# Seven scans ahead of the attention, attention from slot 7, and the feed-forward behind it, in a kernel of two fused layers

## What is computed

```python
xn = layernorm(x)
# layer 0: a selective scan ...
hs, gate = split(xn @ in_proj_w.T)                 # 256 + 256
u  = silu(conv4(hs) + conv_b)
dt, Bm, Cm = rmsnorm of the three parts of u @ x_proj_w.T   # 64, 16, 16
dt = softplus(dt @ dt_proj_w.T + dt_proj_b)
h_t = exp(dt_t * A) * h_{t-1} + (dt_t * u_t) * B_t  # 256 channels x 16 states, over 512 tokens
y  = (sum over states of h * C + u * D) * silu(gate)
x  = x + y @ out_proj_w.T + moe(xn)                 # ... and 8 experts, the best one for each token
xn = layernorm(x)
# layer 1: sliding-window attention (16 heads of 8, |i - j| <= 32) and a gated feed-forward
x  = x + attention(xn) @ Wo + bo + (silu(xn @ wg.T) * (xn @ wu.T)) @ wd.T   # 384 hidden
```

## Time and profile before

| | |
|---|---|
| median of 3 runs | 1098.06 us (1095.71 to 1100.03) |
| profiled execution | 1103.31 us |
| its span | 1101.5 us |
| PE busy | 850.0 us (77%) |
| DVE busy | 763.1 us (69%) |
| ACT busy | 648.3 us (59%) |
| POOL busy | 434.4 us (39%) |
| scans (DVE, 128 of them) | 291.8 us, 2280 ns each |
| mean granted TensorE clock | 0.879 |

### The profile page before, as it was taken

The page is one execution under the profiler, slowest core; times in us unless marked ns, Lnnn a source line. Parts: engine busy times, 40 slices in busy tenths (PEclk is TensorE's granted clock), DMA queues, the critical chain, the costliest instruction groups (busy, mean ns, idle before and its releaser), DMA issues.

```text
span 1101.5 us, 15596 instructions
## 1 busy us (share of the span) xinstructions
PE 850.0 (77%) x5226; PEld 576.7 (52%) x5226; DVE 763.1 (69%) x1059; ACT 648.3 (59%) x1985; POOL 434.4 (39%) x241
## 2 busy tenths in 40 slices
PE   1953888785888878886888787987888788789685
PEld 0731877673644564455445554664456445554443
DVE  7566344556668856895679667856797679878476
ACT  0231556553577637763676567655785577578474
POOL 2256312205732373336433643256226622763000
PEclk9757999986888989998989888898899889889898
DMA  6454888864432442325323542344234423451000
GB/s 226 135 180 124 235 264 272 249 184 96 107 78 68 87 132 70 88 62 143 79 75 79 129 96 63 87 115 104 67 83 117 105 65 82 117 129 40 21 11 10
DMA packets 85951, 123.19 MB, mean 112 GB/s; under 512 B 8560, under 2 KB 43760, under 8 KB 85744
## 3 DMA queue, kind: packets, MB, share of 16 engines
q1 hardware_dynamic: 79584, 115.38, 38.6%
q0 software_dynamic: 6288, 6.82, 2.7%
HBM read 106.21 MB, written 12.29 MB: 108 GB/s over the span
## 4 chain that ended last, share of the span: by engine, by line
PE 40%; DVE 18%; issue 17%; POOL 14%; ACT 8%; DMA 2%; SPq 0%; POOLq 0%; DVEq 0%; ACTq 0%
DVE hst L826 7%; PE more L1451 6%; PE y_bank L1319 6%; POOL hc L1224 6%; PE work L1465 3%; POOL xs_d L1192 3%; PE work L1338 3%; DVE dBu L818 3%; POOL x_res L1208 2%; PE work_l L1433 2%; ACT pexp L1122 2%; PE work L1344 2%; PE work L1364 1%; PE work L1290 1%; PE work L1433 1%
## 5 line engine op out<-in xcount | busy, mean ns | idle before, releaser
L1224 POOL TENSOR_TENSOR hc<-hst,bcr 128x1024 f32<-128x1024 f32 x116 | 281.8, 2429 | 493.2 <-DVE dBu L818 493.2
L826 DVE TENSOR_TENSOR_SCAN hst<-dA,dBu 128x1024 f32<-128x1024 f32 x128 | 291.8, 2280 | 3.3 <-ACT dA L1046 1.8
L1319 PE MATMUL y_bank<-pk,hc 128*128 128x128 f32 x1024 | 154.0, 298 | 54.0 <-POOL hc L1224 50.4
L818 DVE TENSOR_TENSOR dBu<-dtu,bcr 128x1024 f32<-128x1024 f32 x128 | 163.8, 1280 | 35.0 <-DMA bcr<-bc_d 25.7
L1046 ACT ACTIVATE dA<-dt,neg_a 128x511 f32<-128x511 f32 x256 | 170.3, 726 | 12.4 <-DVE hst L826 9.2
L1319 PEld LDWEIGHTS y_bank<-pk,hc 128*128 128x128 f32 x1024 | 126.2, 153 | 89.6 <-POOL hc L1224 60.7
L1451 PE MATMUL more<-pk,pexp 128*96 128x128 f32 x480 | 110.5, 301 | 73.7 <-ACT pexp L1122 68.0
L1451 PEld LDWEIGHTS more<-pk,pexp 128*96 128x96 f32 x480 | 58.9, 129 | 123.4 <-issue 87.8
L1122 ACT ACTIVATE pexp<-work,nmax 128x96 f32<-128x96 f32 x240 | 78.4, 341 | 35.5 <-DVE nmax L973 35.3
L1135 ACT COPY pT<-more 96x512 f32<-96x512 f32 x120 | 69.9, 583 | 44.6 <-PE more L1451 44.3
L1122 ACT ACTIVATE pexp<-work_l,nmax 128x96 f32<-128x96 f32 x240 | 78.1, 340 | 16.5 <-DVE nmax L973 16.4
(11 more groups left out here) (355 smaller groups left out, 1543.4 us busy)
## 6 DMA issues: line engine op xcount, KB each, us to landing
bcr<-bc_d SPq DMA_DIRECT2D x128, 512.0 KB
qbd<-in_wx SPq DMA_DIRECT2D x8, 578.0 KB
o_all<-in_wx SPq DMA_DIRECT2D x8, 578.0 KB
pT<-in_wx SPq DMA_DIRECT2D x8, 578.0 KB
kT<-in_wx SPq DMA_DIRECT2D x8, 578.0 KB, 5.5
vw<-in_wx SPq DMA_DIRECT2D x8, 578.0 KB, 5.7
xs_d<-rbuf POOLq DMA_DIRECT2D x1, 2560.0 KB, 9.7
hst<-in_hidden SPq DMA_DIRECT2D x8, 256.0 KB, 6.6
```

Of the source, the lines that this page charges most:

```text
L818: v.tensor_tensor(dBu[:], dtu[par], bcr[n % RING][:, 0:1, :].to_broadcast([P, NH, L]), ALU.mult).then_inc(s_dBu, 1)
L826: v.tensor_tensor_scan(hst[n % 2][:].rearrange("p h t -> p (h t)"), dA[n % 2][:].rearrange("p h t -> p (h t)"), dBu[:].rearrange("p h t -> ...
L1224: g_.tensor_tensor(hc[n % 2][:], hst[n % 2][:], bcr[n % RING][:, 1:2, :].to_broadcast([P, NH, L]), ALU.mult).then_inc(s_hc, 1)
L1319: last = t.matmul(y_bank[h][:, q], hc[n % 2][:, h, q], ident, is_transpose=True, start=False, stop=(n == N - 1 and j == NT - 1))
```

## The change

The first scans stand in slots 0 to 6, one each, and the others in 8, 10, 12, 14, 16, 18, 20, 23 and 25. Attention begins in slot 7. `HEAD` is gone: the second halves `sg` and `drl` stand in `REST`, a slot after their first halves. The feed-forward stands in slots 24 to 27, and takes the banks of attention (0, 1, 2) in place of bank 5; `fg` k now waits for `fs` k - 1, and `fs` k for `fh` k - 1. The sixteen transfers of `own_heads` are issued four at a time after steps 0 to 3, and the denominators' after the last four. The transfer of k (`kin`) stands a slot later than k, xdbl two slots earlier, the indirect additions into x_res (`rows`) in slots 9 to 15 in place of 5 to 11. The load of ScalarE's ln table is a unit, `ln_set`, in slot 18. The plan of the last turn is unchanged.

```diff
@@ -66,27 +66,26 @@
-ATTN_AT = 10
-STEP_AT = (0, 1, 3, 4, 6, 8, 10, 12, 14, 16, 17, 19, 21, 22, 24, 26)
+ATTN_AT = 7
+STEP_AT = (0, 1, 2, 3, 4, 5, 6, 8, 10, 12, 14, 16, 18, 20, 23, 25)
-HEAD = {11: [("pre", "sg0", 0)], 12: [("pre", "sg1", 0)], 15: [("pre", "drl0", 0)], 16: [("pre", "drl1", 0)],
-        18: [("attn", "fs", 0)], 19: [("attn", "fh", 0)], 20: [("attn", "fs", 1)], 21: [("attn", "fh", 1)],
-MID = {3: [("scan", "slots", 0)], 8: [("pre", "ss", 0)], 19: [("pre", "dw", 0)], 24: [("pre", "dt", 0)], 26: [("pre", "dtu", 0)]}
-REST = {1: [("attn", "x1", 0)],
+MID = {3: [("scan", "slots", 0)], 8: [("pre", "ss", 0)], 20: [("pre", "dw", 0)], 23: [("pre", "dt", 0)], 25: [("pre", "dtu", 0)]}
+REST = {1: [("attn", "x1", 0), ("attn", "ln_a", 0)],
+        4: [("attn", "kin", 0), ("pre", "th1", 0), ("pre", "u1", 0), ("attn", "v0", 0), ("attn", "v1", 0)],
+        24: [("attn", "fg", 0), ("attn", "fu", 0)],
+        25: [("attn", "fs", 0), ("attn", "fh", 0), ("attn", "fg", 1), ("attn", "fu", 1)],
+        26: [("attn", "fs", 1), ("attn", "fh", 1), ("attn", "fg", 2), ("attn", "fu", 2)],
+        27: [("attn", "fs", 2), ("attn", "fh", 2), ("attn", "rden", 0), ("pre", "start", 0)]}
...
@@ -212,9 +208,9 @@
             "values": ["oL" if k == G - 1 else "oK"], "proj": [f"fin{k}"] if k >= 2 else []}.get(name, [])
 
 
-L1_BANK = {"yT0": 1, "yT1": 2, "out": 0, "xnT": 1, "q": 0, "k": 1, "v0": 2, "v1": 0, "v2": 1, "v3": 2, "rdT": 2, "fin": 0,
+L1_BANK = {"yT0": 1, "yT1": 2, "out": 0, "xnT": 1, "q": 0, "k": 1, "v0": 2, "v1": 0, "v2": 1, "v3": 0, "rdT": 2, "fin": 2,
            **{f"s{k}": k % 2 for k in range(G)}, **{f"pT{k}": 2 for k in range(G)},
-           "oL": 0, **{f"gate{k}": 5 for k in range(HC)}, **{f"up{k}": 5 for k in range(HC)}}
+           "oL": 0, "gate0": 1, "up0": 2, "gate1": 0, "up1": 1, "gate2": 2, "up2": 0}
 LAST_BANK = {"yT0": 1, "yT1": 2, "out": 0, "xnT": 1, "q": 3, "k": 4, "v0": 2, "v1": 6, "v2": 7, "v3": 5,
              **{f"s{k}": (0, 1, 3, 4)[k % 4] for k in range(G)}, **{f"pT{k}": (2, 6)[k % 2] for k in range(G)},
              "oK": 0, "oL": 1, **{f"gate{k}": 5 for k in range(HC)}, **{f"up{k}": 7 for k in range(HC)}, "fin2": 5, "fin3": 7}
@@ -481,11 +476,6 @@
 
         def take0(eng, b, key):
             before(eng, s_free0, b * L0_N + L0_USES.index(key))
-            at = BANK0.index(("pre", key))
-            lane, last = BANK0[at - 1]
-            a = b - LAG["attn"] + LAG["pre"] - (at == 0)
-            if lane == "attn" and 0 <= a < B:
-                done1(eng, a, FFN_KEY[last])
 
         def done0(eng, b, key):
             eng.wait_ge(s_free0, b * L0_N + L0_USES.index(key) + 1)
@@ -501,13 +491,6 @@
 
         def take1(eng, b, key):
             before(eng, free1(b, key), l1_before(b, key, l1_bank(b, key)))
-
-        def pre_done(eng, b, name):
-
-            lane, last = BANK0[BANK0.index(("attn", name)) - 1]
-            a = b + LAG["attn"] - LAG["pre"]
-            if lane == "pre" and a < B:
-                done0(eng, a, last)
 
         def done1(eng, b, key):
             if b >= 0:
@@ -602,21 +585,21 @@
                 rows = bc_d[b:b + 1].rearrange("o (k n) t -> o n k t", k=2)
                 sp.dma_start(bcr[n % RING][:], rows[:, n, :, :].to_broadcast([P, 2, L])).then_inc(s_bcr[n % RING], 16)
 
-            def own_heads(b):
-                done1(sp, b, f"gate{HC - 1}")
-                done1(sp, b, "oL")
-                for r in range(RG):
-                    for h in range(4):
-                        q = slice(32 * r + HD * h, 32 * r + HD * h + HD)
-                        sp.dma_start(o_own[q, :], o_all[q, h, :, :].rearrange("p g q -> p (g q)")).then_inc(s_own, 16)
+            def own_head_rows(b, r):
+                if r == 0:
+                    done1(sp, b, f"gate{HC - 1}")
+                    done1(sp, b, "oL")
+                for h in range(4):
+                    q = slice(32 * r + HD * h, 32 * r + HD * h + HD)
+                    sp.dma_start(o_own[q, :], o_all[q, h, :, :].rearrange("p g q -> p (g q)")).then_inc(s_own, 16)
+
+            def averages_of(b):
                 done1(sp, b, "rdT")
                 for r in range(RG):
-                    rows = rd_d[b, r] if isinstance(b, int) else rd_d[bass.ds(b, 1), r].rearrange("o h g q -> (o h) g q")
-                    sp.dma_start(rows.rearrange("h g q -> g h q"), rdenT[r * G:(r + 1) * G, :, :]).then_inc(s_rdst, 16)
+                    sp.dma_start(rd_d[b, r].rearrange("h g q -> g h q"), rdenT[r * G:(r + 1) * G, :, :]).then_inc(s_rdst, 16)
                 sp.wait_ge(s_rdst, b * 64 + 64)
                 before(sp, s_out, b * 16)
-                rows = rd_d[b:b + 1] if isinstance(b, int) else rd_d[bass.ds(b, 1)]
-                sp.dma_start(rd_rows, rows.rearrange("o r h g q -> (o r h) (g q)").unsqueeze(1).to_broadcast(
+                sp.dma_start(rd_rows, rd_d[b:b + 1].rearrange("o r h g q -> (o r h) (g q)").unsqueeze(1).to_broadcast(
                     [RG * 4, HD, L])).then_inc(s_rdin, 16)
 
             def body(it, par):
@@ -631,16 +614,20 @@
                             bc_rows(b, n)
                     if name == "spread" and k + RING - 1 < N:
                         bc_rows(b, k + RING - 1)
-                    if name == "spread" and k == 0 and b >= 2:
-                        own_heads(b - 2)
+                    if name == "spread" and k < RG and b >= 2:
+                        own_head_rows(b - 2, k)
+                        if k == RG - 1:
+                            averages_of(b - 2)
                     if name == "xnT" and (not isinstance(b, int) or b + 1 < B):
                         full0(sp, b, "xnT")
                         sp.wait_ge(s_xast[b + 1], 16)
                         sp.dma_start(x_in[:], seq(xn_d, b + 1)).then_inc(s_xin, 16)
                     if name == "rdT":
                         if b == B - 2:
-                            own_heads(b)
-                    if name == "k" and b < B - 1:
+                            for r in range(RG):
+                                own_head_rows(b, r)
+                            averages_of(b)
+                    if name == "kin":
                         if b == 0:
                             sp.wait_ge(s_clear, 1)
                         done1(sp, b, "k")
@@ -979,6 +966,8 @@
                     v.reciprocal(rden[:], den[:]).then_inc(s_rden, 1)
                 elif name == "fs":
                     dve.wait_ge(s_fth, b * HC + k + 1)
+                    if k > 0:
+                        done1(dve, b, f"up{k - 1}")
                     v.scalar_tensor_tensor(fsg[:], fth[:], 1.0, w1k(b, f"gate{k}")[:], ALU.add,
                                            ALU.mult).then_inc(free1(b, f"gate{k}"), 1)
                 elif name == "fh":
@@ -1076,6 +1065,8 @@
                     act.wait_ge(s_dab, b * NH + NH)
                     done0(act, b, "hs1")
                     s.activation(de, dab, ACT.Exp, scale=-1.0).then_inc(s_de, 1)
+                elif name == "ln_set":
+                    s.preload_act_table_set("natural_log_exp_and_others")
                 elif name == "dln":
                     act.wait_ge(s_dw, b + 1)
                     s.activation(dln, dw, ACT.Ln).then_inc(s_dln, 1)
@@ -1135,9 +1126,9 @@
                     s.copy(pT[k % 4][:], w1k(b, f"pT{k}")[0:KW, :]).then_inc(free1(b, f"pT{k}"), 1)
                 elif name == "fg":
                     full1(act, b, f"gate{k}")
+                    if k > 0:
+                        done1(act, b, f"gate{k - 1}")
                     s.activation(fth[:], w1k(b, f"gate{k}")[:], ACT.Tanh).then_inc(s_fth, 1)
-                    if k == HC - 1 and b < B - 1:
-                        s.preload_act_table_set("natural_log_exp_and_others")
                 elif name == "averages":
                     full1(act, b, "oL")
                     s.copy(o_all[:, :, G - O_LAG:G, :].rearrange("p h g q -> p g h q"),
@@ -1460,8 +1451,6 @@
                 elif name in ("fg", "fu"):
                     key, j = (f"gate{k}", 0) if name == "fg" else (f"up{k}", 1)
                     take1(pe, b, key)
-                    if b < B - 1:
-                        pre_done(pe, b, f"{name}{k}")
                     t.matmul(w1k(b, key)[:], ffn[:, j, k * P:(k + 1) * P], xn1T[:, WIN:WIN + L], start=True,
                              stop=True).then_inc(s_full1, 1)
                 elif name == "rdT":
```

28 lines of the change are left out of this document (10 added, 18 removed).

## The result

The changed kernel takes 1041.66 us (median of 4 runs, 1039.19 to 1043.19), the kernel before 1096.91 in the same job (1095.71 to 1100.03): the ratio is 0.949, 95% interval 0.9461 to 0.9519, some 55 us faster. I had said 1065. The profiled execution took 1043.19 us (span 1041.4), 60.1 less in span than the one of before, where my sum had 33 less.

What follows compares the result with a forecast made beforehand. No engine full; a serial loop through four engines bounds the middle. A turn 37.3 + 52 + 19.1 = 108.4 us; six turns -31, turn 7 -1.4, turn 0 -1.2, together -33: 1065 us, own range 1044 to 1087, 8-in-10 range 1036 to 1100.

Steps and rivals of the forecast that it cites:

- Stretch 1: Slots 0 to 7 with seven scans: 37.3 us, its end set by TensorE, the seventh scan filling VectorE's idle time.
- Stretch 2: Slots 8 to 22, seven scans among the attention's pairs: 52 us, bounds 48 and 56.
- The clean pairs: Middle slots' pairs without feed-forward or other extras, scans 5.16 us apart: 7.5 of them, 38.7 us.
- The preparation with nothing recovered: Middle slots: preparing the next sequence adds 14.7 us to 38.7, 53.4 with no waits of the second halves saved.
- My 11.2 us: The feed-forward's cost between the attention's pairs: 52.5 less 41.3 us, read from turn 7.
- Stretch 3: Slots 23 to 27, from the fifteenth scan to the next turn's first: a VectorE chain of 19.1 us, bounds 18 and 21.
- The clock: TensorE idling in slots 25 to 27 may start the next turn at 1.2 GHz: 0 to 2 us a turn, taken 0.
- Turns -1 and 0: Start of the kernel: turn 0, beside the experts, gains 1.2 us from scan 4; turn -1 unchanged, within 2.
- Turn 7: Last attention turn, preparing nothing: from 88.7 to 87.3 us, -1.4, with product 7's late rows not hidden.
- The loop that keeps 4.2 us a slot: Rival: the four-engine loop sets the attention slots' pace; middle 63 us, turn 119.4, kernel 1136 us; chance 0.12.
- The gap-free TensorE: Rival: TensorE becomes the bound without gaps; 101 to 102 us a turn, kernel 1026 us; chance 0.08.
- The gain spent in tail and start: Rival: clock, a longer tail and late first scores use up the gain; 112 to 114 a turn, 1090 to 1102 us; chance 0.15.

Runs made afterwards that it cites:

- scan7_in_attention: The changed kernel with the seventh scan moved back to slot 8, among the attention's pairs: 1063.7 us, ratio 0.968.
- row7_first: The changed kernel with k's shifted copies (kin) one slot later, in slot 5, behind the transfer of bcr's row 7: 1042.7 us, ratio 0.950.
- halves_ahead: The changed kernel with the second halves of gate and time step back ahead of the next slot's scan, first halves moved too: 1071.7 us, ratio 0.975.
- ffn_middle: The changed kernel with the feed-forward back between the attention's pairs (slots 18 to 24) on its shared bank: 1057.0 us, ratio 0.962.
- eight_scans: The changed kernel with x_dbl in slot 7, kin in slot 5 and the eighth scan in slot 7, ahead of the pairs: 1038.9 us, ratio 0.947.
- filler: eight_scans plus sixteen identity matmuls ahead of pair 11's transposes in each of six turns: 1034.2 us, ratio 0.942.
- xdbl_slot7: The changed kernel with only the x_dbl projection moved from slot 5 back to slot 7: 1036.6 us, ratio 0.944.
- seven_load_later: The changed kernel with x_dbl back in slot 7 and the logarithm's table load in slot 19, seven scans kept ahead: 1034.0 us, ratio 0.942.
- table_load_later: eight_scans with ScalarE's load of the logarithm's table one slot later, in slot 19: 1033.0 us, ratio 0.941.

## Why the prediction was too small

The sign and the mechanism of the packed scans were right; the sizes were not. By parts, predicted and measured in span: to sequence 1 -1.2, -10.3; turns 1 to 6 -31, -49.2; turn 7 -1.4, +0.8; the rest 0, -1.4. A turn was forecast at 108.4 us and takes 105.9 on the mean, 103.1 in the turn that I worked on.

- **Stretch 1, 37.3 predicted, 35.2 measured** (37.1 on the mean, with 43.5 in turn 1). The scans come 3.65 us apart only where nothing else of VectorE's stands between them (558.56 to 562.20, 572.39 to 576.04, 580.63 to 584.28), and 4.1 to 6.1 where the layer norm or the activations do. The fifth product no longer waits, and VectorE has one long wait, 4.67 us. "TensorE sets the end" is shown by scan7_in_attention (same length without the scan) and by row7_first (same length without the wait). The first scores began 33.2 us after the first scan, where I had 35.0. Row 7 was 4.7 us late, not 3; hidden in turns 1 to 6 as said. I had said that it is not hidden in turn 7, where VectorE waits 4.90 us for it; row7_first gained nothing there either (89.6 both), so that step was wrong.
- **Stretch 2, 52 predicted, 49.8 measured: the term that was mis-sized.** The sum had three terms. The clean pairs, 38.7 + 1 in turn 7, were right: the same slots of turn 7 take 39.9 us. The preparation with nothing recovered, 53.4 in all, was nearly right: halves_ahead takes 54.4 on the mean. What I took off for the second halves was wrong: 1.4 us of their 9.0 us of waits, "because everything else in the loop is serial". They are worth 3.8 us in this stretch, in the changed kernel and in the old one, and 4.3 us a turn (halves_ahead), about half. That everything else is serial was no reason to give so little: these waits stood in the series, ahead of the next row maximum. That is 2.9 us a turn more than I took off; turns 1 to 6 gained 3.0 us each more than forecast, and the other misses nearly cancel. The 46 us of TensorE work were too many as well; it was busy for 41.9.
- **The feed-forward.** My 11.2 us are no term of the sum above, but they gave the move its size. In the middle it costs 6.2 us on the mean, somewhat more without the table load's move, and 8.7 in turn 7. With the 4.5 us that it costs in the tail, and 0.5 in stretch 1, its move gives 1.1 us a turn on the mean (ffn_middle), and not the 6 that my rows implied.
- **Stretch 3, 19.1 predicted, 18.1 measured.** A VectorE chain, as said; fs 0 didn't wait, and the feed-forward's idle was 0.3 us where I had 1.2.
- **The clock.** I feared up to 12 us of loss and took 0. In the middle stretches of turns 1 to 6 it rose, by 0.04 on the mean (0.87 to 0.91), 0.11 in the turn shown. Why isn't shown: with the second halves' waits back it is 0.91 on the mean too. The Trainium skill's rule ("TensorE: Matmul & The Clock Gate", clock gate) that idling brings the half-rate back is borne out by eight_scans and filler (3.13 us of waiting, then 0.73; no waiting, then 1.00). I looked for the idling only where the change adds it, and not inside the pairs. How much of the 49 us is the clock I did not separate; filler's 1.1 us a turn (turns 2 to 6) is for one such gap.
- **Turns -1 and 0, the other missed part, 9 us.** The table of slots is the same for all turns, so its edits also act there. x_dbl two slots earlier gave 4.2 us at the first scan, 2.4 at sequence 1 (xdbl_slot7); the second halves, between the experts' tiles, 4.6 (halves_ahead), or 5.3 in turn 0 of the old kernel (161.6 against 167.0). I had only counted a scan.
- **Heads in four parts.** Right in kind; worth 9 to 11 us by itself, which I had not priced apart.
- **Turn 7, 87.3 predicted, 89.6 measured.** The changed kernel, xdbl_slot7 and seven_load_later do the same in this turn (it prepares nothing and loads no table), and have 89.6, 87.2 and 90.5 in their profiled executions. So the miss of 2.3 us is no larger than what one execution differs from another by.
- **The rivals.** The loop that keeps 4.2 us a slot: no, 3.3. The gap-free TensorE at 101 to 102 a turn, 1026 us: 1041.7 is nearer to it than to 1065, but a part of that is the start, and TensorE still waited 5.6 us in the middle; table_load_later reaches 100.6 in single turns. The gain spent in tail and start: no. 1041.7 lies a little below the range of the forecast's own case, 1044 to 1087, and inside the wide one only because that made room for the fast rival. (The chances for faster add up to 0.78, not 0.79.)

## What to carry over

In a loop that passes through several engines, price a wait by what stands behind it on the waiting engine: where that was the loop's next hand-over, about half of 9.0 us came back in every turn; where another engine's longer chain ran beside it, nothing did, even of 4.7 us. And when a schedule's table serves all stages, go through every stage with it, the warm-up too; then undo each edit by itself, as one of them (here x_dbl) may work against the rest.

## What the runs showed of the hardware

- The granted clock depends on TensorE's waits within a stretch, but not on their length alone. In eight_scans a wait of 3.13 us was followed by matmuls at half rate in each of six turns (0.73 each time), and in filler, with the gap filled, by none in five (1.00). The wait of 2.80 us in the changed kernel and xdbl_slot7 was followed by 0.73, 0.85 or 1.00, and the stretch took 12.5, 11.65 and 10.60 us. The wait of 1.71 us in table_load_later was followed by 0.84 or by 1.00. This goes with much of what makes turns with equal work differ by up to 2.6 us (103.1 to 105.7): the longer ones have this stretch at 0.73 or the pairs behind the eighth scan at 0.84.
- Useless matmuls in such a gap paid: 3.84 us of them, 1.6 us shorter.
- The sixteen float32 matmuls of 128x128 in filler are 32 in the trace, 0.12 us each at full clock; a float32 transpose of 128x128 is one (the eight of a y sum are x8).
- dBu on VectorE took 2.34 us (586.96) where GpSimd's product with the averages ran from 586.95 to 588.21, and takes 1.23 alone: it is 1.11 longer, nearly that product's 1.26. The kernel before had 1.87, 0.64 longer, with the product's last 0.78 us beside it. This is the lock of the port pair that the prediction named (the Trainium skill, "SBUF — State Buffer", Terms), here nearly in full. The scans did not lengthen: between 540 and 880 us of the changed kernel sixteen of them began while GpSimd's hc ran, and took 2.27 or 2.28 us.
